# Folding a 512-code search in pairs: difference scores, a ScalarE clip, and a 256-column VectorE search

## What is computed

```python
x = x + conv_block(group_norm(x))            # Haar transform, 12 convolutions, inverse Haar
xn = group_norm(x).reshape(-1, 32)           # one vector of 32 per position
dists = sum(xn ** 2) - 2.0 * xn @ codebook.T + sum(codebook ** 2)   # codebook: 512 x 32
x = x + codebook[argmin(dists)]
```

## Time and profile before

| | before |
|---|---|
| median of 3 runs | 2001.28 us (2001.2, 2001.28, 2004.69) |
| profiled execution, span | 1999.1 us |
| PE busy | 1852.8 us (93%) |
| VectorE busy | 1753.1 us (88%) |
| ScalarE busy | 1025.9 us (51%) |
| GpSimd busy | 1259.2 us (63%) |
| chain that ended last, by engine | PE 53%, DVE 29%, POOL 7%, ACT 5%, issue 5% |
| PE clock by slice | 9 or 10 tenths of full speed until 1800 us, 5 tenths in the tail |

### The profile page before, as it was taken

The page is one execution under the profiler, slowest core; times in us unless marked ns, Lnnn a source line. Parts: engine busy times, 40 slices in busy tenths (PEclk is TensorE's granted clock), DMA queues, the critical chain, the costliest instruction groups (busy, mean ns, idle before and its releaser), DMA issues.

```text
span 1999.1 us, 22686 instructions
## 1 busy us (share of the span) xinstructions
PE 1852.8 (93%) x6112; PEld 1114.6 (56%) x6112; DVE 1753.1 (88%) x3923; ACT 1025.9 (51%) x2058; POOL 1259.2 (63%) x1363
## 2 busy tenths in 40 slices
PE   7999999999999999999999999999999999985553
PEld 5654666456754666556754666556754666432221
DVE  5312799999999999999999999999999999989896
ACT  3325464746456464656456464656456453634331
POOL 1001267756777567766777567766677567767876
PEclk8999999999999999999999999999999999995555
DMA  6621463234532463234532463234532463201111
GB/s 190 186 79 48 111 154 99 71 92 117 157 80 69 116 156 104 71 84 128 156 82 70 116 155 104 72 85 128 154 83 54 112 154 90 60 19 34 37 37 32
DMA packets 135024, 197.21 MB, mean 99 GB/s; under 512 B 36977, under 2 KB 82545, under 8 KB 134897
## 3 DMA queue, kind: packets, MB, share of 16 engines
q1 hardware_dynamic: 101808, 178.40, 31.9%
q0 software_dynamic: 32768, 16.84, 5.4%
q10 hardware_dynamic: 320, 0.52, 0.1%
HBM read 117.52 MB, written 23.72 MB: 71 GB/s over the span
## 4 chain that ended last, share of the span: by engine, by line
PE 53%; DVE 29%; POOL 7%; ACT 5%; issue 5%; ACTq 0%; DMA 0%; POOLq 0%; DVEq 0%
PE ring L961 44%; DVE idx L1503 11%; DVE top L1499 10%; PE score L886 6%; POOL vqc L1618 5%; ACT yst L1118 2%; PE score L818 1%; DVE bands L1325 1%; ACT ha L1034 1%; POOL vqc L1632 1%; DVE brs L1388 1%; DVE ha L1388 1%; DVE bands L1443 1%; ACT hb L1034 1%; DVE bands L1439 1%
## 5 line engine op out<-in xcount | busy, mean ns | idle before, releaser
L1618 POOL DMA_INDIRECT vqc<-in_codebook,idx x1024 | 999.8, 976 | 447.9 <-DVE idx L1503 243.5
L1499 DVE MAX8 top<-score 128x8 f32<-128x512 f32 x1024 | 689.1, 683 | 50.1 <-PE score L886 31.3
L1503 DVE FIND_INDEX8 idx<-top,score 128x8 uint32<-128x512 f32 x1024 | 701.9, 689 | 0.0
L886 PE MATMUL score<-cst,yst 98*128 98x512 f32 x1024 | 619.7, 611 | 88.6 <-DVE idx L1503 70.6
L961 PE MATMUL ring<-hfp,wring 128*128 128x512 f32 x2160 | 594.1, 409 | 3.0 <-ACT hfp L1192 3.0
L961 PEld LDWEIGHTS ring<-hfp,wring 128*128 128x128 f32 x2160 | 409.1, 190 | 116.6 <-issue 10.8
L1118 ACT CAST yst<-bands 32x256 fp32r<-32x256 f32 x1024 | 411.7, 402 | 92.2 <-PE score L886 79.9
L961 PE MATMUL ring<-ha,wfull 128*128 128x512 f32 x896 | 439.1, 597 | 5.9 <-POOL ha L1650 5.2
L886 PEld LDWEIGHTS score<-cst,yst 98*128 98x128 f32 x1024 | 204.6, 202 | 293.8 <-DVE idx L1503 175.0
L961 PE MATMUL ring<-hb,wfull 128*128 128x512 f32 x736 | 356.6, 595 | 0.0
L961 PEld LDWEIGHTS ring<-ha,wfull 128*128 128x128 f32 x896 | 168.6, 190 | 150.3 <-issue 126.6
(11 more groups left out here) (138 smaller groups left out, 1362.0 us busy)
## 6 DMA issues: line engine op xcount, KB each, us to landing
wring<-wparts SPq DMA_DIRECT2D x119, 384.0 KB, 3.4
hfp<-hfp SPq DMA_DIRECT2D x96, 255.0 KB, 5.1
yst<-yl SPq DMA_DIRECT2D x512, 32.0 KB
vqc<-in_codebook,idx POOLq DMA_INDIRECT x1024
out<-vqc SPq DMA_DIRECT2D x128, 128.0 KB
xnat<-in_x SPq DMA_DIRECT2D x112, 128.0 KB
wfull<-in_weights SPq DMA_DIRECT2D x32, 384.0 KB, 3.6
sidep<-hfp SPq DMA_DIRECT2D x96, 127.5 KB, 3.2
```

What stands on the lines that cost most here:

```text
L886: nc.tensor.matmul(score[bank][:, :], yst[0:KST, j % 2, g, wp], cst[0:KST, :], start=True, stop=True).then_inc(s_tile, 1)
L1499: nc.vector.max(top8[:, t % 4, :], score[bank][:, :]).then_inc(s_top, 1)
L1503: nc.vector.max_index(idx[:, t // CTILES % 2, t % CTILES, :], top8[:, t % 4, :], score[bank][:, :]).then_inc(s_idx, 1)
L1618: nc.gpsimd.indirect_dma_start(vqc[:, c % 2, w * CH:(w + 1) * CH], None, codebook[:, :], bass.IndirectOffsetOnAxis(idx[:, c % 2, k, 0:1], ...
```

## The change

The 512 codes are folded into 256 pairs (k, k + 256). In the stacked codes the second half of the columns now holds the code of k + 256 minus that of k, so one score matmul yields 256 scores of the low codes and 256 difference scores. Per tile ScalarE clips the differences at zero into a buffer in SBUF (`rise`), VectorE adds them to the low scores and takes the maximum of the sums in one instruction with an accumulator (`maximum`), and then searches 256 columns in SBUF for it (`index`). This gives the pair. PE's bank is released by `s_top` (after `maximum`) and no longer by `s_idx`.

Which code of the pair it is, is chosen later: a table in DRAM (`pairs`, two copies) has a row of 97 floats per pair: both codes, their difference with the present scale, and a threshold. Per image two matmuls, a ScalarE copy and two DMAs write the last 33 columns (`table`, a new turn at the boundary). The gather fetches 97 floats per position into `picked` (three slots of 8 tiles). Per 8 tiles VectorE multiplies the difference by the position's values, sums, compares with the threshold and overwrites where the upper code wins (`select`, four instructions); POOL then adds 128 x 256 in place in `ync`, twice per 16 tiles, and SP stores from `ync`.

To make room in SBUF `pside` is laid over `sidep`, which needs new memsets on POOL and two waits on PE and ACT (`s_flank`, `s_shore`). `mean1` and `var1` share a bank, so that the table can have a turn. The costs and the table of `spread_turns` are the same but for the new entry ("table", 17.6).

The core of the diff:

```diff
-PRIMED = 1
+PAIRS = CODES // 2
+HALVES = TILES // JTILES
+ROW = 3 * CH + 1
+SLOTS_G, SLOTS_R = 3, 3
...
-BOUNDARY = [("mean2", 6.9), ("var2", 9.3), ("scale2", 13.5), ("bias2", 16.9)]
+BOUNDARY = [("mean2", 6.9), ("var2", 9.3), ("scale2", 13.5), ("bias2", 16.9), ("table", 17.6)]
...
                     if what == "tile" and 1 <= b <= IMAGES:
-                        return pe.wait_ge(s_idx, TILES * (b - 1) + k + 1)
+                        return pe.wait_ge(s_top, TILES * (b - 1) + k + 1)
...
+            def table(v):
+                pe.wait_ge(s_cbs, v + 1)
+                for i in range(2):
+                    t = nc.tensor.matmul(score[BANK["table",]][:, P * i:P * i + CH + 1],
+                                         cbs[:, PAIRS + P * i:PAIRS + P * (i + 1)], factors[:, 0:CH + 1],
+                                         start=True, stop=True)
+                t.then_inc(s_tabled, 1)
...
+            def rise(v, t, bank):
+
+                n = TILES * v + t
+                act.wait_ge(s_tile, n + 1)
+                wait(act, s_idx, n + 1 - SLOTS_R)
+                nc.scalar.activation(best[:, n % SLOTS_R, :], score[bank][:, PAIRS:CODES], ACT.Relu)\
+                    .then_inc(s_rise, 1)
...
+                    elif v > 0 and what == "late":
+                        rise(v - 1, step[1], BANK[step])
                     elif quant and what == "tile":
+                        rise(v, step[1], BANK[step])
...
             def maximum(v, t, bank):
+                n = TILES * v + t
                 if t % CTILES == 0:
-                    c = t // CTILES
-                    wait(dve, s_add, PRIMED + XCHUNKS * v + c - 1)
-                wait(dve, s_tile, TILES * v + t + 1)
-                nc.vector.max(top8[:, t % 4, :], score[bank][:, :]).then_inc(s_top, 1)
+                    wait(dve, s_add, HALVES * v + t // JTILES - 2)
+                dve.wait_ge(s_rise, n + 1)
+                nc.vector.tensor_tensor_reduce(
+                    out=best[:, n % SLOTS_R, :], in0=score[bank][:, 0:PAIRS], in1=best[:, n % SLOTS_R, :], scale=1.0,
+                    scalar=-ABSENT, op0=ALU.add, op1=ALU.max, accum_out=top8[:, t % 4, 0:1]).then_inc(s_top, 1)
...
+            def select(v, q):
...
+                dve.wait_ge(s_gather[n % SLOTS_G], 128 * (n // SLOTS_G + 1))
+                after(nc.vector.tensor_tensor(prod[:, :, :], rows[:, :, 2 * CH:3 * CH], y, ALU.mult), s_lean, 3 * n + 1)
+                after(nc.vector.tensor_reduce(lean[:, 0, :], prod[:, :, :], AXIS.X, ALU.add), s_lean, 3 * n + 2)
+                after(nc.vector.tensor_tensor(lean[:, 1, :], lean[:, 0, :], rows[:, :, 3 * CH], ALU.is_gt),
+                      s_lean, 3 * n + 3)
...
+                nc.vector.copy_predicated(rows[:, :, 0:CH], upper, rows[:, :, CH:2 * CH]).then_inc(s_select, 1)
...
+                        if t % JTILES == 4 and t > JTILES:
+                            select(n, t // JTILES - 1)
+                        if what == "tile" and t == 2 and n:
+                            select(n - 1, HALVES - 1)
...
             def gather(v, t):
-                c, k = t // CTILES, t % CTILES
-                if k == 0:
-                    pool.wait_ge(s_store[c % 2], PRIMED + 32 * ((XCHUNKS // 2) * v + c // 2))
-                wait(pool, s_idx, TILES * v + t + 1)
-                w = 8 * (k // JTILES) + 2 * (k % BLK) + k % JTILES // BLK
+                c, k, n = t // CTILES, t % CTILES, HALVES * v + t // JTILES
+                if t == 0:
+                    wait(pool, s_static, 64)
+                    pool.wait_ge(s_table, 32 * (v + 1))
+                if t % JTILES == 0:
+                    wait(pool, s_add, n + 1 - SLOTS_G)
+                pool.wait_ge(s_idx, TILES * v + t + 1)
+                w = 2 * (k % BLK) + k % JTILES // BLK
                 nc.gpsimd.indirect_dma_start(
-                    vqc[:, c % 2, w * CH:(w + 1) * CH], None, codebook[:, :],
-                    bass.IndirectOffsetOnAxis(idx[:, c % 2, k, 0:1], 0)).then_inc(s_gather[c % 2], 16)
+                    picked[:, n % SLOTS_G, w * ROW:(w + 1) * ROW], None, pairs[v % 2][:, :],
+                    bass.IndirectOffsetOnAxis(idx[:, c % 2, k, 0:1], 0)).then_inc(s_gather[n % SLOTS_G], 16)
```

More of the change, by code:

```diff
@@ L10 @@
 U32 = mybir.dt.uint32
+AXIS = mybir.AxisListType
 P = 128
@@ L173 @@
 STARTS, SPREAD = bank_turns()
-TURNS = [x for x, _ in STARTS if x[0] not in ("var2", "scale2")] + SPREAD
+ORDERED = [x for x, _ in STARTS] + SPREAD
+TURNS = [x for x in ORDERED if x[0] not in ("var2", "scale2", "var1")]
 assert len(TURNS) % BANKS == 0
@@ L177 @@
 BANK["var2",] = BANK["mean2",]
+BANK["var1",] = BANK["mean1",]
 HAAR_AT = {c * CTILES + (XTURN if c < XCHUNKS - 1 else LASTX) + XDELAY - 1: c for c in range(XCHUNKS)}
-RUN_ENDS = [x[1] for x, y in zip(TURNS, TURNS[1:] + [("end",)]) if x[0] in ("tile", "late")
+RUN_ENDS = [x[1] for x, y in zip(ORDERED, ORDERED[1:] + [("end",)]) if x[0] in ("tile", "late")
             and (x[1] in (*HAAR_AT, NORMAL_AT, MAIN_TILES - 1, TILES - 1) or y[0] in ("mean1", "var1"))]
@@ L710, in _ @@
                 sp.dma_start(dst[:, :], src[:, :]).then_inc(s_const, 16)
+            for rows in pairs:
+                for h in range(2):
+                    sp.dma_start(rows[:, h * CH:(h + 1) * CH], codebook[h * PAIRS:(h + 1) * PAIRS, :])\
+                        .then_inc(s_static, 16)
             def stack(v, j):
@@ L777, in body @@
                         stack(v, 1)
+                    elif quant and what == "table":
+                        table(v)
                     elif quant and what == "tile":
@@ L986, in body @@
                         bias2(v)
+                    elif quant and what == "table":
+                        bank_free(b, step)
+                        table(v)
                     elif quant and what == "ychunk":
@@ L1098, in mean_factors @@
                 wait(act, s_bias, v)
-                nc.scalar.activation(factors[0:CH, :], idn[0:CH, :], ACT.Identity, bias=mall[1][0:CH, :], scale=0.0)\
+                wait(act, s_tabled, v)
+                nc.scalar.activation(factors[0:CH, CH:CH + P], idn[0:CH, :], ACT.Identity, bias=mall[1][0:CH, :],
+                                     scale=0.0)\
                     .then_inc(s_neg, 1)
@@ L1224, in body @@
                         bias_parts(v)
+                    elif quant and what == "table":
+                        table_rows(v)
+                    elif v > 0 and what == "late":
+                        rise(v - 1, step[1], BANK[step])
                     elif quant and what == "tile":
+                        rise(v, step[1], BANK[step])
                         j, k = step[1] // JTILES, step[1] % JTILES
```

138 lines of the change are left out of this document (98 added, 40 removed).

## The result

| | before | after |
|---|---|---|
| median of the runs | 2001.24 us (4 runs, 1998.7 to 2004.69) | 2167.22 us (4 runs, 2162.64 to 2168.75) |
| profiled execution | 2001.3 us, span 1999.1 | 2168.29 us, span 2166.2 |
| mean granted clock of PE | 0.945 | 0.928 |

The change makes the kernel slower: ratio 1.0829, 95% interval 1.0812 to 1.0846. The forecast was slower, 2071 us with a range up to 2118. So the sign held, and the size (+70 forecast, +166 measured) did not.

What follows compares the result with a forecast made beforehand. PE was taken to bound a round and POOL the tail. From 2001.3 us, 29.4 + 18.9 + 17.4 + 10.2 - 11.9 + 6.1 = +70.1 gave 2071 us; forecast 2056 to 2092, wider range 1992 to 2118.

Steps and rivals of the forecast that it cites:

- What bounds the kernel: Rounds: PE bounds, busy 221.66 of 224.97 us, VectorE close behind with 217.37; POOL bounds the tail.
- waits coming back: Rounds: PE's waits for VectorE's index, 7.1 us, shrink by 1.7 per round, seven times: -11.9 us.
- Prices: New operations: clip 0.43 us, maximum 0.42 start-to-start, search 0.42, selection 1.5; gather issue on POOL unchanged.
- rival 2: Gathers: longer rows cost 0.25 us more on each of 1,024, total 2115 us; chance 0.10.
- The tail's term: Tail: its boundary +3.3, table copy and DMA +1.7, last selection less half an add +1.1: +6.1 us.
- Boundary: Round boundaries: clip and selection delay tile 0 by 3.3 us, slower clock 1.6; 4.9 six times, +29.4 us.
- the dip of the clock: Boundary: after PE's longer idle, 4 us at granted clock 0.59 instead of 1.00, losing 1.6 us each time.
- ScalarE's blocks: After w12 and at wd1: clips queued behind ScalarE's copies and casts, +2.7 seven times (+18.9), +2.9 six times (+17.4).
- The last norm: End of a round: selection at tile 116 waits for gather 111 to land, +1.7 us six times, +10.2.
- Rival 3: Rounds: VectorE's relief removes all index waits, 50 us, and clips find ScalarE free: 1977 us; chance 0.15.

Runs made afterwards that it cites:

- e9: The changed kernel without ScalarE's clip, VectorE adding a constant table instead, selections kept: 1994.67 us, ratio 0.9966.
- e10: The changed kernel without both the clip (constant table instead) and the choice within a pair: 1970.01 us, ratio 0.9843.
- e2: The changed kernel without the choice within a pair (no selections; GpSimd waits for the gather itself), clips kept: 2094.01 us.
- e6: The changed kernel with all clips done by VectorE ahead of its add and maximum, ScalarE doing nothing per tile: 2091.07 us.
- e7: The changed kernel with the clips of 28 tiles behind ScalarE's long blocks done by VectorE, the other 100 by ScalarE: 2073.27 us.
- e13: The changed kernel with ScalarE's instruction per tile cut to one column, its place and waits kept, VectorE adding a constant table: 2132.48 us.
- e14: The changed kernel with 52 tiles' clips on VectorE, selections two tiles later, two placed as in e12: 2103.79 us, ratio 1.0511.
- e12: The kernel of e7 with two selections later (tile 116 to 119, the one ahead of scale to next round's tile 1): 2058.78 us.

## Why the prediction was right and wrong

**What bounds the kernel: right, and underused.** PE bounds a round. e9 and e10 show it: with VectorE's work cut to 178 and 161 us, rounds are 224.6 and 221.5. Of the forecast's -11.9 for waits coming back, 1.7 per round, only 21-41 shows some in the change, 0.7 us per round; without clip and choice 3.7 us per round came back.

**Prices: right** to 0.05 us for clip, maximum, search; the selection was 1.5 us (446 + 420 + 174 + 481 ns). A gather of 97 floats costs no more POOL time (rival 2 false, 1.25 us). The add of half a chunk took 752 ns where half of 1.27 us had been assumed. The tail's term was 6.1 us and measured 3.2; one of its parts was summed too high, a selection of 1.5 less half an add being 0.9 and not 1.1.

**Boundary: right in mechanism, and the sum in part by luck.** `scale` came 4.9 us later against the last sum (5.1 forecast), the dip of the clock was there, the sum 5.4 (4.9 forecast). Two errors cancel in it: in the four rounds of the table PE's idle time grew by 2.6 us (3.3 forecast), and its busy time, at the lower clock, by 2.8 (1.6 forecast).

**ScalarE's blocks: the step that failed.** The term was mis-sized: 2.7 and 2.9 us forecast, 5.4 and 7.6 measured, over seven and six rounds some 47 of the 96 us by which the sum was short. It took the blocks from the trace before as they stood, and added one clip and one maximum behind them. PE's waits for these maxima came out near the forecast, 3.3 and 2.7 us per round. Three things beside them were left out:

- PE's clock falls after a long wait here as well, though it was priced only at the boundary. In 14-21 PE's busy time grew by 2.2 us with a mean granted clock of 0.87, and in 79-88 by 2.0. Over a whole round what the granted clock lacks adds up to 6.8 us at the full clock.
- A block starts later when VectorE is late: 1.35 to 1.70 instead of 0.3 us after tile 14. Without the selections it is 0.3 again (e2), so it is the selection ahead of `ha` that does this. The forecast gave a selection a price only at the boundary, before the last norm and at the end of the tail.
- VectorE's work for the convolutions comes late too. In 79-88 PE waited 2.7 us per round for `ha` and `hb`. The 2.42 us at 1139.76 are such a wait: `hb` (1138.40) stood in VectorE's queue behind a selection (1134.16) and the sums of the next image. The wait can run in a circle, VectorE behind clips, ScalarE's result copies behind clips that wait for indices or scores (207.8 and 139.6 us), VectorE's next work for the convolutions behind these; how much goes round it is argued from these waits and not measured.

**Between the blocks: a term that was missing.** 41-79 and 88-118 lost 2.7 and 1.2 us, over seven rounds some 27 us. The forecast had nothing there. In 41-79 it takes clips and selections together: without either one nothing is lost (58.1 in e2, 57.7 in e9, 58.2 before). In 88-118 the clips do it (47.6 in e2, 45.0 in e9). The single waits are of 0.5 to 1.1 us.

**The last norm: half the size, and luck in it.** 3.4 us against 1.7. The forecast's mechanism, a selection that waits for its gathers, is not what held PE in the change: the selection waited for nothing (1189.85), and clips 116 and 117 stood behind squares and side copies. It is what happens without the clips (e9, 3.02 us of waiting, 9.7 in the table). The clips alone (e2) cost as much as clips and selection together, 10.3; with neither (e10) it is 6.9. So each of the two causes is enough, and the one does not add to the other.

**Rival 3 (faster)** had 50 us to come back. e9 gives 7 and e10 31. It took its 50 us from the weight loads' rows, which overlap the matmuls; PE's own idle time, 3.3 us of a round, 23 in seven, was nearer to what could be had.

The Trainium skill's rule in Perfetto Trace Analysis, section Optimizing Scalar/DVE Operations, that moving work off a saturated DVE may pay, did not help here. VectorE was busy but not the bound, so its relief, with the selections that it brings, was worth 7 us (e9), and the step in ScalarE's queue cost 173.

The Trainium skill (ScalarE: Activation LUTs, section Rules for kernel authors) would have a relu on VectorE. All clips on VectorE gave 2091 instead of 2167 us (e6), and 28 of 128 there gave 2073 (e7). The gain came from the queue and not from a faster clip, which lasted 409 ns on VectorE and 380 on ScalarE.

What stays open: how the 138 us of e13 divide. Between e9 and e13 a round grows by 20.8 us, of which 11.9 are idle time of PE and 8.9 longer busy time, and the lower clock accounts for some 7 of it; but how much of the waiting is the circle and how much the plain place behind a block is not shown. Nor is why e14 fell behind e12: it lost 4.3 us per round in 88-118, 2.0 in 41-79 and 1.6 in 21-41.

## What to carry to other kernels

Here a step on another engine cost what its queue cost, not what it lasts: 0.38 us of ScalarE per tile made 173 us. So before an instruction is put between a producer and the release of a buffer, ask for every place in that engine's order what stands ahead of it, what stands behind it, and whether one of those is what the producer needs. Take the bound engine's own idle time as a first estimate of what relieving a second engine can give (here 3 us of 225), and try the relief with the new work left out before building the rest. Where two in-order queues wait for each other, delays can add up to more than their sum, as clip and selection did here by 49 us; a sum of delays read from a trace in which the queues didn't wait for each other was too low for that reason.
